# Four column tiles for the router product of a chunk, and one transpose in place of four

## The reference, cut to what matters

```python
x = x + tanh(g_xattn) * xattn(layernorm(x), ctx)     # 16 heads of 32, causal, 100 keys are ever seen
h = layernorm(x)                                     # 1600 x 512
route = sigmoid(h @ router_w)                        # 1600 x 8: one logit for each of 8 experts
e = argmax(route, axis=1);  p = max(route, axis=1)
x = x + tanh(g_ffn) * p * (silu(h @ gate_w[e]) * (h @ up_w[e])) @ down_w[e]
```

## Time and profile before

| what | value |
|---|---|
| median of three runs | 558.25 us |
| profiled execution, its own time | 560.19 us |
| span of it, first to last instruction | 558.7 us |
| TensorE matmul busy | 508.5 us, 91% |
| TensorE weight load busy | 423.9 us, 76% |
| VectorE, ScalarE, GpSimd busy | 349.5, 303.6, 185.4 us |
| mean granted TensorE clock | 0.965 of full speed |

### The profile page before, as it was taken

One profiled execution on the slowest core, in us unless ns is written; L12 is line 12 of the kernel. 1 busy time (PEld: TensorE's weight loads), 2 busy tenths in 40 slices (PEclk: granted clock), 3 DMA queues, 4 the chain that ended last, 5 costly groups with the idle time before them and its releaser, 6 DMA issues.

```text
span 558.7 us, 11407 instructions
## 1 busy us (share of the span) xinstructions
PE 508.5 (91%) x3724; PEld 423.9 (76%) x3724; DVE 349.5 (63%) x745; ACT 303.6 (54%) x855; POOL 185.4 (33%) x210
## 2 busy tenths in 40 slices
PE   0999999999999999976489999999999999999991
PEld 0976686768665866656489999999999999999980
DVE  3678568756885556686446666757566665766731
ACT  0799648765786568522134554545454644545520
POOL 5534304631572147233532233224122241220211
PEclk9999999999999999995599999999999999999996
DMA  7500032103310031073428676887677797776610
GB/s 195 169 8 2 16 90 88 61 16 90 89 48 25 15 91 59 18 245 115 104 81 246 212 237 184 262 248 210 199 240 220 212 283 205 205 244 195 224 54 29
DMA packets 58910, 77.30 MB, mean 138 GB/s; under 512 B 5074, under 2 KB 40506, under 8 KB 58880
## 3 DMA queue, kind: packets, MB, share of 16 engines
q1 hardware_dynamic: 53728, 66.90, 40.2%
q0 software_dynamic: 5152, 10.03, 6.3%
HBM read 67.76 MB, written 10.34 MB: 140 GB/s over the span
## 4 chain that ended last, share of the span: by engine, by line
PE 71%; DVE 8%; issue 7%; ACT 6%; POOL 3%; DMA 3%; DVEq 0%; ACTq 0%; SPq 0%; POOLq 0%
PE bank L1148 20%; PE bank L1149 20%; PE bank L1150 19%; ACT pr L668 3%; POOL pn L508 3%; PE bank L1243 2%; PE bank L1233 2%; DMA staging<-in_L_xattn_Wq 2%; PE bank L1282 1%; PE bank L1402 1%; PE bank L1252 1%; ACT staging L612 1%; PE bank L1169 1%; PE bank L1290 1%; DVE pT L970 1%
## 5 line engine op out<-in xcount | busy, mean ns | idle before, releaser
L1148 PE MATMUL bank<-x_hi,gu_hi 128*128 128x224 f32 x512 | 142.6, 279 | 2.9 <-ACT qT L744 1.6
L1149 PE MATMUL bank<-x_lo,gu_hi 128*128 128x224 f32 x512 | 141.9, 277 | 0.0
L1150 PE MATMUL bank<-x_hi,gu_lo 128*128 128x224 f32 x512 | 140.3, 274 | 0.0
L1148 PEld LDWEIGHTS bank<-x_hi,gu_hi 128*128 128x128 f32 x512 | 99.2, 194 | 4.6 <-ACT qT L744 1.7
L1149 PEld LDWEIGHTS bank<-x_lo,gu_hi 128*128 128x128 f32 x512 | 99.2, 194 | 1.0
L1150 PEld LDWEIGHTS bank<-x_hi,gu_lo 128*128 128x128 f32 x512 | 99.3, 194 | 0.0
L668 ACT ACTIVATE pr<-bank,nmx 100x100 f32<-100x100 f32 x256 | 85.6, 374 | 15.5 <-DVE nmx L961 12.1
L781 DVE TENSOR_TENSOR gu_lo<-staging,gu_hi 128x1024 fp32r<-128x1024 f32 x64 | 76.6, 1221 | 16.7 <-ACT gu_hi L612 15.6
L612 ACT ACTIVATE gu_hi<-staging 128x1024 fp32r<-128x1024 f32 x64 | 65.7, 1050 | 31.9 <-DMA staging<-in_L_ffn_up_w 20.7
L508 POOL TENSOR_TENSOR pn<-pr,inv 100x400 f32<-100x400 f32 x64 | 54.6, 853 | 77.7 <-DVE inv L954 72.5
L668 ACT ACTIVATION_READ_ACCUMULATOR pr<-bank,nmx 100x1 f32 x256 | 60.2, 236 | 0.0
(11 more groups left out here) (182 smaller groups left out, 963.7 us busy)
## 6 DMA issues: line engine op xcount, KB each, us to landing
staging<-in_L_ffn_gate_w SPq DMA_DIRECT2D x32, 512.0 KB, 5.4
staging<-in_L_ffn_up_w SPq DMA_DIRECT2D x32, 512.0 KB, 7.2
staging<-in_L_ffn_down_w SPq DMA_DIRECT2D x32, 512.0 KB, 4.0
x_rows<-x SPq DMA_DIRECT2D x8, 800.0 KB
xt<-in_x SPq DMA_DIRECT2D x4, 800.0 KB
xr<-in_x SPq DMA_DIRECT2D x16, 200.0 KB
staging<-in_L_xattn_Wq SPq DMA_DIRECT2D x1, 1024.0 KB, 11.5
x<-in_L_xattn_Wout SPq DMA_DIRECT2D x1, 1024.0 KB, 9.7
```

The source lines that it names most:

```text
L1148: nc.tensor.matmul(dst, a[0], b[0], start=first, stop=False)
L1149: nc.tensor.matmul(dst, a[0], b[1], start=False, stop=False)
L1150: return nc.tensor.matmul(dst, a[1], b[0], start=False, stop=last)
```

## The change

The router weights get a second copy, `router_wide` (128 x 4 x 32), with 8 columns of weights and 24 of zeros in each group. The logits are computed as four column tiles of the array, tile i for batch i of the chunk: 16 products, each with 128 x 32 loaded and 100 columns moving, into partitions 32i to 32i+31 of the bank. So the exponential works on 128 x 100, and one 128 x 100 transpose replaces four of 8 x 100; VectorE reads its 4 x 8 columns out of 4 x 32. On GpSimd there is a memset of `router_wide` among the constants and a copy from `router` behind the first four token normalisations; TensorE waits for that copy ahead of the first keys.

```diff
+        router_wide = sb("router_wide", [P, KC, HD], F32)
...
-        ex_t = sb("ex_t", [E, CT], F32)
+        ex_t = sb("ex_t", [P, S], F32)
...
-                self.logits = bank[0:E, first * S:stop * S]
+                self.logits = bank[:, 0:S]
+                self.turned = bank[0:S, P:P + CB * HD]
+                self.chosen_from = self.turned.rearrange("p (i h) -> p i h", h=HD)[:, :, 0:E]
...
-        CONSTS = 19
+        CONSTS = 20
...
+            nc.gpsimd.memset(router_wide[:], 0.0).then_inc(consts, 1)
-            pool.wait_ge(consts, 7)
+            pool.wait_ge(consts, 8)
...
             for i in range(CB):
                 normalise_tokens(0, i)
+            pool.wait_ge(small_loaded, 48)
+            nc.gpsimd.tensor_copy(router_wide[:, :, 0:E], router[:]).then_inc(router_widened, 1)
             pool.wait_ge(w_turned, 6)
...
-                    add(nc.vector.tensor_scalar(ex[0:S, b], part.ex if part is whole else ex[0:S, b], 1.0, None, ALU.add))
+                    add(nc.vector.tensor_scalar(ex[0:S, b], part.chosen_from if part is whole else ex[0:S, b], 1.0, None, ALU.add))
...
                 for k in range(KC):
-                    ins = nc.tensor.matmul(whole.logits, router[:, k, :], x2T[:, k, :], start=k == 0, stop=k == KC - 1)
+                    for i in range(CB):
+                        ins = nc.tensor.matmul(whole.logits[i * HD:(i + 1) * HD, :], router_wide[:, k, :],
+                                               x2T[:, k, i * S:(i + 1) * S], start=k == 0, stop=k == KC - 1,
+                                               tile_position=(0, i * HD), skip_group_check=True)
                 ins.then_inc(logits_ready.sem, 1)
...
-                for i in range(CB):
-                    ins = nc.tensor.transpose(whole.ex_b[i], ex_t[:, i * S:(i + 1) * S], ident[0:E, 0:E])
-                ins.then_inc(ex_ready.sem, 1)
+                nc.tensor.transpose(whole.turned, ex_t[:], ident[:]).then_inc(ex_ready.sem, 1)
...
             pe.wait_ge(small_loaded, 48)
+            pe.wait_ge(router_widened, 1)
```

More of the change, by code:

```diff
@@ L265, in flamingo_block @@
         consts = sem("consts")
+        router_widened = sem("router_widened")
         tanh_done = sem("tanh_done")
```

## The result

The changed kernel takes 552.69 us (median of four, 552.27 to 553.80) against 559.28 us for the kernel before in the same comparison (four executions, 558.22 to 561.51). The ratio is 0.988 with a 95% interval of 0.9842 to 0.9918. So the kernel is faster, clear of the noise; that it is so by more than 1% is likely and not certain, for the interval reaches past 0.99. The forecast of 553.4 us held as a time, but it stood on the median of 558.25 us, and the fourth execution lifted that to 559.28. The predicted gain of 4.83 us stands against 6.6 us measured.

A forecast was written before the change was run, and what follows sets the result against it. TensorE's queue was taken as the bound. Gains of 1.45 + 1.45 + 1.93 = 4.83 us in the three later attends, off the 558.25 us median, gave 553.42 us, range of 8 in 10 from 551.5 to 557.0 us.

The forecast's parts named there:

- The product: Router's product in three attends: 0.83 us, priced from weigh, in place of 2.79 us in TensorE's queue.
- What is late next in attend(1) and (2): Behind the router, pn's transposes would wait for pn, leaving 1.45 us gained in each of these attends.
- Attend(3): Last attend: pn needed directly behind the router is long done, so 1.93 us gained, no idle TensorE.
- The transpose of the logits: One 128 x 100 transpose for four small ones: nothing, bounds 0.28 us gained to 0.17 us lost per chunk.
- The exponential: Router's exponential on ScalarE, 128 x 100 for 8 x 400: 0.13 us less at most, worth nothing to the time.
- The beginning: New memset and copy on GpSimd at the start: hidden, nothing lost, with 0 to 0.2 us as a bound.
- the rival that held it: Whole saving and more, if pn's chain moves, logits' transpose vanishes, clock returns sooner: 6.7 us gained, 551.5 us; chance 0.21.
- The serial tiles: Router's column tiles run one after the other, adding into the same PSUM columns: 10.2 us slower, 568.5 us; chance 0.04.
- the bare loads: Router's weight loads stand alone, not overlapped: 3.42 us per product, 1.9 us lost in all, 560.1 us; chance 0.04.
- the gain dying at the turn of the chunk: In attend(1) and (2) a transfer sets the turn of the chunk; only attend(3) gains 1.93 us, 556.3 us; chance 0.10.
- The clock: Behind the attention, the return from half clock could lose or gain 2.4 us; counted in the range only.
- the stretch at half clock takes another length: Sign of a wrong prediction: the half-clock stretch behind the attention changes its length; no size given.

The follow-up runs named there:

- e4: Changed kernel with the two loops of the router's product exchanged, all four pieces of one column tile before the next: 555.62 us.
- e3: Kernel before with the router's product cut into 16 pieces of 100 columns, all in one place of the array, no column tiles: 561.31 us, ratio 1.0027.
- e2: Changed kernel with the one 128 x 100 transpose of the logits issued four times into the same place: 555.19 us.
- e5: Changed kernel without the wide copy of the router weights, its memset and its wait; each tile loads 128 x 8: 553.16 us, ratio 0.9873.
- e6: Changed kernel with the projection of batch 1 ahead of the transposes of tile 12 in attend(1) and (2): 553.32 us, ratio 0.9867.
- e1: Changed kernel run again without an edit, beside the kernel before: 553.80 us against 559.68 us, ratio 0.9898.
- e10: Kernel before, instructions unchanged, ex_t laid out behind all other tensors so that what follows has the changed kernel's addresses: 560.06 us, ratio 0.9999.
- e11: Changed kernel with router_wide laid out last and a gap behind ex_t, so every other tensor has its address of before: 554.63 us, ratio 0.9893.

## Why the prediction was right, and where it was not

**The product** (0.83 us): 0.83, 0.82 and 0.81 us. The shape that the kernel already had gave the price. The rule of the Trainium skill (TensorE: Matmul & The Clock Gate, Part 3, The mechanism) by which the loads would stand bare, weighed there against the trace, doesn't hold here either: 32 loads of 106 to 113 ns lie within 0.67 us, though all four tiles share their rows. The high bound of 6.2 us, where each record pays its load and its columns one after the other, is far from anything seen: tile by tile it was 1.92 us (e4), without tiles 2.85 (e3).

**What is late next in attend(1) and (2)** (1.45 us each): 3.67 - 2.24 = 1.43 and 3.67 - 2.23 = 1.44 us. The wait of some 0.4 us was there with 0.37. **Attend(3)** (1.93 us): 1.97 us, all of it from the product. No idle time ended by pn was forecast there; 0.16 us came, one tile behind the place that was looked at.

**The transpose of the logits** (nothing, bounds 0.28 gained to 0.17 lost): this step was mis-sized. It gained 0.21 us in attend(1) and in attend(2). In attend(3) it gained at its place and was lost again in the wait for pn, 0.31 us each way. That makes the 0.4 us of 5.22 - 4.83. The reason given for it, that most of the cost is the way in and out, is wrong: e2 shows 0.11 us for each further transpose of the large form.

**The exponential** (0.13 us less): 0.26 for 0.48 us, 0.22 less and so beyond the bound, and without effect, as said. **The beginning** (nothing): the memset took 0.21, the copy 0.22 us, and TensorE and ScalarE weren't delayed: the context's transposes start at 17.27 us in e5, without both, and at 16.98 in e6, with both.

**What was missed:** the change moves the tensors laid out behind router_wide and ex_t to other addresses, and this is worth about 0.8 us in the loop over units, half of the span (282.85 of 558.7 us from the first gate product on; "two thirds" ahead of the prediction is too much), which the prediction passed over. With 5.2 and 0.8 us the sum is 6.0 us, and the two comparisons of the changed kernel gave 6.6 and 5.9 us between medians. That fits, but the 0.8 us is shown for the loop and not for the whole time.

**The chances:** 0.75 went to a gain under 1%, 0.21 to more. The ratios, 0.988 and then 0.9898, lie just on the side that had the 0.21, with intervals that reach over to the other. Of the three parts of the rival that held it, one came: most of the transposes' cost vanished in attend(1) and (2). The chain of pn stayed, and by e1 the clock is play and no part of the gain. The rest came of the addresses, which no rival had. The serial tiles, the bare loads and the gain dying at the turn of the chunk were all wrong; the stretches between rank and the next router are the same to 0.03 us.

**The clock** was rightly held to be play, not gain: in these traces the part from the last weigh to the first gate product runs from 32.65 to 33.99 us over kernels that issue the same instructions there. But the prediction named as a sign of being wrong that "the stretch at half clock takes another length", and it did: 27.3 for 30.7 us in the profile of the changed kernel. e1's reading shows that this sign was badly chosen, for the length varies without the change. It also helped the profiled span: 8.1 us between the two, where the medians have 6.6.

## What to carry to other kernels

Look for a product with a small stationary operand and many moving columns: here 8 loaded columns with 400 moving took 2.79 us, and the same work cut over four column tiles 0.83. Give neighbouring instructions to different tiles, for tile by tile it was 1.92 us, and take the price from a place where the kernel has that shape already. Then ask which chain ran beside the old, longer work: here it kept 0.5 us of 1.96 twice, and an exchange in the queue gave that back in the traces. When a layout changes, compare the period of every untouched loop before crediting the edit.

## What the runs showed of the hardware that was not expected

- The order of the column tiles: 32 records, four tiles in turn, 0.83 us; the same records tile by tile, 1.92 us; all in one place, 2.85 us.
- A float32 transpose in a run of four costs 0.11 us in the queue with 100 loaded and 128 moving columns (the further ones of e2), 0.07 with 8 moving ones (a quarter of the 0.28 us before); the single large one of the changed kernel 0.07 us in attend(1) and (2), 0.11 in attend(3).
- The same float32r products take 33.22 or 33.33 us per turn by where tensors lie in SBUF, a difference of 0.3%. In the stretch from 300 to 500 us the products with wq_lo have a mean of 397 ns in the kernel before and 390 in the changed one. The row of the kernel before, then of the changed one, of e10 and of e11, from the grouped lines (count, busy us, mean ns):

```profile
L1149 PE MATMUL bank<-wq_lo,wkv_hi 128*112 128x512 f32 x97 | 38.5, 397 | 0.0
```

```profile
L1156 PE MATMUL bank<-wq_lo,wkv_hi 128*112 128x512 f32 x97 | 37.9, 390 | 0.0
```

```profile
L1151 PE MATMUL bank<-wq_lo,wkv_hi 128*112 128x512 f32 x97 | 37.9, 390 | 0.0
```

```profile
L1158 PE MATMUL bank<-wq_lo,wkv_hi 128*112 128x512 f32 x96 | 38.0, 396 | 0.0
```
